# Relative attention: own scores of four units in one group, or of two pairs around the first transposes

## The chip, the cores and the metric

The kernel runs on one core of one Trainium2 chip. The metric is the device time of one execution, in microseconds (us). The profile comes from one more execution, taken by the hardware profiler; its span is the time from the first to the last instruction of the program.

## What is computed

The reference is a two-layer decoder on x of 4 batches x 512 positions x 128 features, in float32: per layer an attention, a cross attention and a feed-forward part with experts. Here one stage matters, the second layer's attention with relative positions: 16 heads of size 8, 512 queries and keys in each of 4 batches. In short:

```python
score_1 = einsum('bhqd,bhkd->bhqk', q_head, k_head)
score_2 = einsum('qmd,qkd->qmk', q_resh, rpk)      # rpk: rel_k by clipped distance q - k
scores  = (score_1 + score_2) / sqrt(D)
attn    = softmax(scores)
weight_1 = einsum('bhqk,bhkd->bhqd', attn, v_head)
weight_2 = einsum('qmk,qkd->qmd', se, rpv)         # rpv: rel_v by clipped distance
out = (weight_1 + weight_2) @ Wo.T + bo
```

## The kernel before

The program is written per engine: each engine has its own list of instructions in a fixed order, and semaphores (the table SD) hold them to each other. Stages A to G follow one another; stage D, the relative attention, is `pe_D` on TensorE, `act_D` on ScalarE, `dve_D` on VectorE and `pool_D` on GpSimd.

Stage D handles four units at a time. Q counts these groups, 16 to a batch (w = Q % 16) and 64 in all. A unit k = 4Q + j has its scores, 128 rows x 512 keys in float32, in one PSUM bank, and the banks go round in a ring of five: unit k has bank k % 5. So a unit's scores may be written only when the exp of unit k - 5 has read them.

TensorE does four things for a group, in `pe_D`:

- `scores(Q)`: 16 matmuls of the own scores (L1159), each on one 32x32 tile of the array. `e` is the unit, `c` the 32 output rows, and the input rows are `r = c ^ e`, so the 16 matmuls lie on 16 different tiles. Then four matmuls of the relative scores (L1169), two pairs (`par`), one unit on each half of the rows, which add into the same banks. Their semaphore `sc` tells VectorE that a pair is done. In front stands one wait: `exp` >= 4Q - 1, that is, until the third unit of the group before has been read.
- `flips(Q, 0)` and `flips(Q, 1)`: 16 transposes each (L1185), of the exps of the first and of the second pair of units. Each waits until the earlier half's transposes have been copied out, by ScalarE (`pta`) and by VectorE (`ptv`).
- `values(Q)`: 32 matmuls with the values (L1209) and 16 or 24 with the relative values (L1223).

The loop issues `scores(Q + 1)`, `flips(Q, 0)`, `values(Q - 1)`, `flips(Q, 1)`, one group ahead with the scores and one behind with the values. Once a batch, at w = 1, `spread_own` (L1239) and `spread_other` (L1251) come in, and the values move to the end.

ScalarE (L1279, L1290) does, for each Q: exp of unit 4Q+4, copy of the first transposes, exp of 4Q+5 and 4Q+6, copy of the second transposes, exp of 4Q+7. VectorE (L1321, L1329) does: top (negated maximum of a unit's scores) of 4Q+4 and 4Q+5, copy of the first transposes, top of 4Q+6, on even Q `pick` (L1337, L1341: two multiplies that take the values out of PSUM), top of 4Q+7, on even Q `add` (L1351), copy of the second transposes. Both take their half of each transposed block from its own PSUM bank. No DMA stands in this loop, except loads for the next batch on SP's queue.

Of the kernel before, what the change touches and what calls it, by code (L numbers as in the profile page):

```python
# [11 lines left out]
P = 128  # L12
B = 4
S = 512
# [30 lines left out]
RK0 = DK * (NU - 1) - REL0  # L45
# [43 lines left out]
def decoder(nc, t, out, last="G"):  # L89
# [3 lines left out]
    with ctx:  # L93
        def sb(name, shape, dt=F32):
            return ctx.enter_context(nc.sbuf_tensor(name, shape, dt))

        def sem(name):
            return ctx.enter_context(nc.semaphore(name))

        ps = ctx.enter_context(nc.psum_tensor("ps", [P, 8, 512], F32))  # L100
# [3 lines left out]
        w = {n: sqw[:, i, :] for i, n in enumerate(SQW)}  # L104
# [26 lines left out]
        rk = sb("rk", [P, RKW])  # L131
# [831 lines left out]
        def pool_C(pool):  # L963
# [8 lines left out]
            for n in range(NTT):  # L972
# [5 lines left out]
        SD = {n: sem("s_d_" + n) for n in ("qsp", "kst", "ldk", "ldv", "kp", "kt", "qt", "v", "spill", "ld", "a", "rk", "rv", "sc", "max", "exp", "t", "pta",  # L978
                                           "ptv", "pv", "oex", "sum", "rin", "ee", "r", "yn", "y2", "yst", "ao", "at")}
# [4 lines left out]
        NW = NU // 4  # L984
# [4 lines left out]
        AI = [a.rearrange("p (u n) -> p u n", u=QD) for a in (cw[:, 0:E1 * HID1],  # L989
                                                            cw[:, E1 * HID1:2 * E1 * HID1])]  # L990
# [16 lines left out]
        def unit_D(w, j):  # L1007

            z = j % 2
            return (2 * w + j // 2 if z == 0 else NU - 2 - 2 * w + j // 2), z  # L1010

        def tiles_D(w, z):

            n = 2 if w < NW // 2 else 3
            return list(range(n)) if z == 0 else list(range(NT - 1, NT - 1 - n, -1))

        NQ = B * NW
# [125 lines left out]

        def pe_D(pe):

            def scores(Q):
                b, w = Q // NW, Q % NW
                if w == 0:
                    if b:
                        pe.wait_ge(SD["ld"], LD * b)  # L1150
                    else:
                        pe.wait_ge(SD["ldk"], 32)
                    pe.wait_ge(SD["a"], 5 * (b + 1) + 1)
                if Q >= 1:
                    pe.wait_ge(SD["exp"], 4 * Q - 1)
                for e in range(4):
                    for c in range(4):
                        r, j = c ^ e, e
                        nc.tensor.matmul(ps[GW * c:GW * (c + 1), (4 * Q + j) % 5, :],  # L1159
                                         ALL[b % 2][GW * r:GW * (r + 1), j % 2, j // 2 * NW + w, :, :],  # L1160
                                         KT[b % 2][GW * r:GW * (r + 1), :], start=True, stop=False, skip_group_check=True,
                                         tile_position=(GW * r, GW * c))
                for par in range(2):
                    for z in range(2):
                        j = 2 * par + z
                        u = unit_D(w, j)[0]
                        k0, k1 = (0, min(S, 8 * u + 8 + P)) if z == 0 else (8 * u - P, S)
                        r0 = k0 - 8 * u + (RK0 if z == 0 else P)
                        nc.tensor.matmul(ps[:, (4 * Q + j) % 5, k0:k1], AI[b % 2][64 * z:64 * z + 64, par * NW + w, :],  # L1169
                                         rk[64 * z:64 * z + 64, r0:r0 + k1 - k0], start=False, stop=True,  # L1170
                                         skip_group_check=True).then_inc(SD["sc"], 1)

            def flips(Q, h):

                m = 2 * Q + h
                if m >= 1:
                    pe.wait_ge(SD["pta"], m)
                    pe.wait_ge(SD["ptv"], m)
                for j in range(2):
                    k = 2 * m + j  # L1180
                    pe.wait_ge(SD["exp"], k + 1)
                    for i in range(NT):
                        for z in range(2):
                            rows = slice(64 * z, 64 * z + 64)
                            ins = nc.tensor.transpose(ps[:, TB[z], j * 256 + i * 64:j * 256 + i * 64 + 64],  # L1185
                                                      PB[k % 6][rows, i * P:(i + 1) * P], c["ident"][rows, rows],
                                                      tile_position=(64 * z, 0))
                            if i == NT - 1:
                                ins.then_inc(SD["t"], 1)

            def values(Q):
                b, w = Q // NW, Q % NW
                q0 = 128 * (Q % 2)
                pe.wait_ge(SD["pta"], 2 * Q + 2)
                pe.wait_ge(SD["ptv"], 2 * Q + 2)
                if Q == 0:
                    pe.wait_ge(SD["ldv"], 16)
                    pe.wait_ge(SD["rv"], 2)
                if w == 0 and b >= 1:
                    pe.wait_ge(SD["yn"], 4 * b)  # L1200
                elif Q % 2 == 0 and Q:
                    pe.wait_ge(SD["oex"], Q)
                for h in range(2):
                    for t in range(NT):
                        for g in range(4):
                            j0, j1 = 2 * h, 2 * h + 1
                            m = PT[:, Q % 2, j0, t * P + GW * (g ^ j0):t * P + GW * (g ^ j0) + 1]
                            step = S + GW * (g ^ j1) - GW * (g ^ j0)
                            nc.tensor.matmul(ps[GW * g:GW * (g + 1), OBK, q0 + 64 * h:q0 + 64 * h + 64],  # L1209
                                             VT[b % 2][:, t * P + GW * g:t * P + GW * (g + 1)],  # L1210
                                             bass.AP(m.tensor, m.offset, [list(m.ap[0]), [step, 2], [1, GW]]),
                                             start=(t == 0), stop=(t == NT - 1), skip_group_check=True,
                                             tile_position=(0, GW * g))
                near = [tiles_D(w, z) for z in range(2)]
                n = len(near[0])
                for par in range(2):
                    for t in range(n):
                        for x4 in range(4):
                            z, ih = x4 // 2, x4 % 2
                            j = 2 * par + z  # L1220
                            u = unit_D(w, j)[0]
                            t0 = z * RVZ + (8 * u + S - P - P * near[z][t] - RV0) * DK + ih * GW
                            ins = nc.tensor.matmul(ps[GW * x4:GW * (x4 + 1), OBK, 256 + q0 + 64 * par:256 + q0 + 64 * par + 64],  # L1223
                                                   rv[:, t0:t0 + GW],
                                                   PT[:, Q % 2, j, near[z][t] * P:(near[z][t] + 1) * P]
                                                   .rearrange("p (h i) -> p h i", h=H)[:, :, 4 * ih:4 * ih + 4],
                                                   start=(t == 0), stop=(t == n - 1), skip_group_check=True,
                                                   tile_position=(0, GW * x4))
                            if t == n - 1 and par == 1:
                                ins.then_inc(SD["pv"], 1)  # L1230
# [15 lines left out]
            def spread_other(b):  # L1246

                pe.wait_ge(SD["ee"], 2 * b + 2)
                pe.wait_ge(SD["yn"], 4 * b + 1)
                for z in range(2):  # L1250
                    nc.tensor.matmul(ps[64 * z:64 * z + 64, OBK, :], rmask[:, :], E2R[:, z * S:(z + 1) * S],  # L1251
                                     start=True, stop=True, skip_group_check=True).then_inc(SD["r"], 1)

            scores(0)
            for Q in range(NQ):
                if Q + 1 < NQ:
                    scores(Q + 1)
                done = Q // NW - 1 if Q % NW == 1 and Q > 1 else None
                flips(Q, 0)
                if done is not None:  # L1260
                    spread_own(done)
                elif Q >= 1:
                    values(Q - 1)
                flips(Q, 1)
                if done is not None:
                    spread_other(done)
                    values(Q - 1)
# [1145 lines left out]
```

## Time and profile before

| | |
|---|---|
| time, median of 3 runs | 1510.87 us (1509.27 to 1512.24) |
| the profiled execution: its time | 1513.77 us |
| the profiled execution: its span | 1512.0 us |
| TensorE, VectorE, ScalarE busy, share of the span | 83%, 66%, 48% |
| granted clock of TensorE, mean | 0.93 |
| stage D | from 413 to about 812 us |

A busy share is a mean over seven stages with different limits. What a change in one stage is worth is read from that stage: from a table of stretches inside it, from the time line of one iteration, and from what ended the idle time of the engine in question. "issue" names idle time of an engine that waited for nothing that the profile shows. Ends of matmuls are modelled; their starts are recorded, so the text goes from start to start.

### The profile page before, as it was taken

Reading aid. Unit: us, or ns where it says so; the run is one execution under the profiler, and the core shown is the slowest. Engines: PE = TensorE matmul, PEld = TensorE weight load, DVE = VectorE, ACT = ScalarE, POOL = GpSimd, SP = SyncE. Lnnn points to the kernel's source line nnn. Section 1 sums busy time; section 2 is a strip of 40 time slices with the busy share of each in tenths; the row PEclk is TensorE's granted clock in tenths of the full one; section 3 lists DMA queues with packets and bytes.
Section 4 is the critical chain, followed back from the end, with each engine's and each line's share of the span. In section 5 each row is a group of like instructions: output and inputs, shape, how many; then the busy total and the mean of one; then the engine's idle time right before and its main releaser. Section 6 shows DMA issues by size and latency. Waiting matters only on the chain.

```text
span 1512.0 us, 46849 instructions
## 1 busy us (share of the span) xinstructions
PE 1250.1 (83%) x19471; PEld 796.5 (53%) x19471; DVE 991.6 (66%) x2513; ACT 730.2 (48%) x1814; POOL 236.7 (16%) x216
## 2 busy tenths in 40 slices
PE   4888888696479899898994889888988898889755
PEld 3443434285246666666663346634763476357544
DVE  4576676522558777777773678687858785778533
ACT  1323141442156666666661429543944394439334
POOL 2011121123030103131002030004000400030035
PEclk8989998898779999999996999999998999899878
DMA  9700000011440010110003200000000000000031
GB/s 323 286 8 9 17 1 8 9 55 46 157 159 4 11 39 5 26 24 11 11 5 80 53 1 2 4 1 15 3 4 1 14 3 2 1 15 3 4 101 49
DMA packets 56628, 59.27 MB, mean 39 GB/s; under 512 B 27854, under 2 KB 42065, under 8 KB 55265
## 3 DMA queue, kind: packets, MB, share of 16 engines
q1 hardware_dynamic: 51872, 47.82, 10.0%
q0 software_dynamic: 2528, 5.27, 1.1%
q8 instruction: 155, 2.54, 0.7%
q10 hardware_dynamic: 2016, 3.18, 0.6%
q14 instruction: 57, 0.46, 0.1%
HBM read 32.56 MB, written 24.14 MB: 38 GB/s over the span
## 4 chain that ended last, share of the span: by engine, by line
PE 54%; DVE 18%; ACT 11%; issue 8%; SPq 3%; DMA 3%; POOL 2%; ACTq 0%; POOLq 0%; DVEq 0%
PE ps L1159 5%; PE ps L271 5%; PE ps L1169 5%; DVE arena L620 4%; PE ps L1577 4%; PE ps L1185 4%; PE ps L492 3%; DVE arena L1730 3%; ACT arena L1668 3%; PE ps L1209 3%; PE ps L518 3%; DVE arena L1740 2%; PE ps L1632 2%; ACT arena L1678 2%; ACT arena L1279 2%
## 5 line engine op out<-in xcount | busy, mean ns | idle before, releaser
L1321 DVE TENSOR_REDUCE nmax<-ps 128x1 f32<-128x512 f32 x256 | 166.5, 682 | 70.4 <-PE ps L1169 70.4
L1668 ACT ACTIVATE arena<-ps,arena 128x512 f32<-128x512 f32 (+3 forms) x256 | 134.7, 539 | 74.4 <-DVE arena L1730 71.4
L1279 ACT ACTIVATE arena<-ps,nmax 128x512 f32<-128x512 f32 x172 | 118.9, 695 | 70.6 <-DVE nmax L1321 69.8
L1730 DVE TENSOR_REDUCE arena<-ps 128x1 f32<-128x512 f32 (+3 forms) x256 | 115.6, 484 | 15.1 <-PE ps L1592 13.5
L620 DVE TENSOR_REDUCE arena<-ps 128x8 f32<-128x1232 f32 x64 | 88.9, 1437 | 30.6 <-PE ps L480 30.6
L1329 DVE COPY arena<-ps 128x512 f32<-128x512 f32 x128 | 87.2, 682 | 22.5 <-PE ps L1185 22.3
L1740 DVE TENSOR_SCALAR arena<-arena 128x512 f32<-128x512 f32 (+3 forms) x256 | 92.0, 391 | 5.7
L1678 ACT COPY arena<-ps 128x512 f32<-128x512 f32 x160 | 85.9, 597 | 12.5 <-PE ps L1607 12.5
L271 PE MATMUL ps<-identb 128*128 128x512 bf16 x336 | 90.3, 428 | 1.4 <-DVE kcol L754 1.4
L1587 PE MATMUL ps<-arena 64*128 64x384 f32 (+3 forms) x512 | 88.3, 456 | 0.0
L1623 PE MATMUL ps<-arena 128*64 128x128 f32 x1280 | 87.8, 279 | 0.0
L1607 PE MATMUL ps<-sqc,arena 64*128 64x64 f32 x1280 | 67.1, 235 | 24.4 <-ACT arena L1678 11.4
L1290 ACT COPY arena<-ps 128x512 f32<-128x512 f32 x128 | 74.6, 583 | 24.7 <-PE ps L1185 23.4
L634 DVE TENSOR_TENSOR arena<-arena 128x512 f32<-128x512 f32 x96 | 62.8, 717 | 34.7 <-ACT arena L595 34.6
L1169 PEld LDWEIGHTS ps<-rk,cw 64*128 64x128 f32 x512 | 44.5, 192 | 61.0 <-issue 56.4
L1607 PEld LDWEIGHTS ps<-sqc,arena 64*128 64x128 f32 x1280 | 51.6, 138 | 46.1 <-ACT arena L1678 30.0
L1169 PE MATMUL ps<-rk,cw 64*128 64x168 f32 (+25 forms) x512 | 75.7, 414 | 0.0
L1623 PEld LDWEIGHTS ps<-arena 128*64 128x64 f32 x1280 | 68.5, 137 | 6.4
L1185 PE MATMUL ps<-sqc,arena 64*128 64x64 f32 x1376 | 62.7, 229 | 9.9 <-issue 7.1
L1159 PE MATMUL ps<-tmp,arena 32*32 32x512 f32 x1024 | 43.1, 642 | 31.4 <-DVE cw L1422 19.2
L475 PE MATMUL ps<-arena,q_t 32*128 32x320 f32 x512 | 52.5, 479 | 19.4 <-DVE arena L620 11.4
L1185 PEld LDWEIGHTS ps<-sqc,arena 64*128 64x128 f32 x1376 | 55.5, 142 | 21.2 <-issue 11.0
(354 smaller groups left out, 2574.5 us busy)
## 6 DMA issues: line engine op xcount, KB each, us to landing
xs_d<-onehot SPq DMA_DIRECT2D x4, 2560.0 KB, 26.4
cw<-in_cw SPq DMA_DIRECT2D x2, 2048.0 KB, 11.6
rv<-in_rv SPq DMA_DIRECT2D x2, 1536.0 KB, 16.5
late<-in_gw SPq DMA_DIRECT2D x3, 1024.0 KB, 10.6
arena<-gs_d SPq DMA_DIRECT2D x23, 129.0 KB, 2.1
onehot<-q_s SPq DMA_DIRECT2D x96, 8.0 KB
arena<-xs_d SPq DMA_DIRECT2D x23, 64.0 KB, 1.8
xs_d<-arena SPq DMA_DIRECT2D x23, 64.0 KB, 1.6
```

What stands on the lines that cost most here:

```text
L271: nc.tensor.matmul(ps[:, FILL[k][1], :].rearrange("p (a n) -> p a n", a=NT), identb[:, :], identb[:, :].unsqueeze(1).to_broadcast([P, NT, ...
L620: nc.vector.tensor_reduce(top_x[:, i, :, 2 * hp:2 * hp + 2], ps[:, bank:bank + NG4, 0:2 * KP].rearrange("p g (h k) -> p g h k", h=2)[:, :, ...
L1159: nc.tensor.matmul(ps[GW * c:GW * (c + 1), (4 * Q + j) % 5, :], ALL[b % 2][GW * r:GW * (r + 1), j % 2, j // 2 * NW + w, :, :], KT[b % 2][G ...
L1169: nc.tensor.matmul(ps[:, (4 * Q + j) % 5, k0:k1], AI[b % 2][64 * z:64 * z + 64, par * NW + w, :], rk[64 * z:64 * z + 64, r0:r0 + k1 - k0], ...
L1185: ins = nc.tensor.transpose(ps[:, TB[z], j * 256 + i * 64:j * 256 + i * 64 + 64], PB[k % 6][rows, i * P:(i + 1) * P], c["ident"][rows, row ...
L1279: nc.scalar.activation(PB[k % 6], ps[:, k % 5, :], ACT.Exp, bias=nmax[:, u:u + 1], accum_out=rsum[:, b % 2, u:u + 1]).then_inc(SD["exp"], 1)
L1321: nc.vector.tensor_reduce(nmax[:, k % NU:k % NU + 1], ps[:, k % 5, :], AX.X, ALU.max, negate=True)\
L1607: ins = nc.tensor.transpose(ps[:, FTB[z], (NT * h + j) * KD:(NT * h + j + 1) * KD], TF["p%d" % (n % 2)][HALVES[z], h * S + j * P:h * S + ( ...
L1623: ins = nc.tensor.matmul(ps[HALVES[h], FOB[a % 2], i * P:(i + 1) * P], TF["v"][:, v0:v0 + KD], PTF[n % 2][h][:, c0 + j * P:c0 + (j + 1) * ...
L1668: ins = nc.scalar.activation(TF["p%d" % (n % 2)][:, h * S + c0:h * S + c1], ps[:, FSB[n % 2][h], c0:c1], ACT.Exp, bias=TF["nmax"][:, k8:k8 ...
L1730: ins = nc.vector.tensor_reduce(TF["nmax"][:, k8:k8 + 1], ps[:, FSB[n % 2][h], c0:c1], AX.X, ALU.max, negate=True)
L1740: ins = nc.vector.tensor_scalar(p[:, c0:c1], p[:, c0:c1], TF["rinv"][:, k8 + k:k8 + k + 1], None, ALU.mult)
```

## The change

`scores` takes a second argument, `par`, and does the own and the relative scores of one pair of units. The loop issues the first pair where the whole group stood, and the second pair between the values and the second transposes. Each pair waits for the exps that its own two banks need: count 4Q - 3 and count 4Q - 1.

```diff
-            def scores(Q):
+            def scores(Q, par):
                 b, w = Q // NW, Q % NW
-                if w == 0:
+                if w == 0 and par == 0:
...
-                if Q >= 1:
-                    pe.wait_ge(SD["exp"], 4 * Q - 1)
-                for e in range(4):
+                if Q:
+                    pe.wait_ge(SD["exp"], 4 * Q + 2 * par - 3)
+                for e in (2 * par, 2 * par + 1):
                     for c in range(4):
                         r, j = c ^ e, e
                         nc.tensor.matmul(ps[GW * c:GW * (c + 1), (4 * Q + j) % 5, :],
...
-                for par in range(2):
-                    for z in range(2):
-                        j = 2 * par + z
...
+                for z in range(2):
+                    j = 2 * par + z
...
-            scores(0)
+            scores(0, 0)
+            scores(0, 1)
             for Q in range(NQ):
                 if Q + 1 < NQ:
-                    scores(Q + 1)
+                    scores(Q + 1, 0)
                 done = Q // NW - 1 if Q % NW == 1 and Q > 1 else None
                 flips(Q, 0)
                 if done is not None:
                     spread_own(done)
                 elif Q >= 1:
                     values(Q - 1)
+                if Q + 1 < NQ:
+                    scores(Q + 1, 1)
                 flips(Q, 1)
```

## Rows read from the trace of the kernel before

**Rows 1.** The page, busy us, share of the span and instructions of each engine.

```profile
PE 1250.1 (83%) x19471; PEld 796.5 (53%) x19471; DVE 991.6 (66%) x2513; ACT 730.2 (48%) x1814; POOL 236.7 (16%) x216
```

**Rows 2.** Table by stretch: length, PE and PEld of L1159; last row all lines.

```profile
530.40:617.30 86.90, 20.05 (x480) 4.16 (x480) 1.00 0.09 19
626.70:709.80 83.10, 18.51 (x480) 3.92 (x480) 1.00 0.09 20
719.80:788.80 69.00, 15.99 (x384) 3.28 (x384) 1.00 0.04 8
...
sum 239.00, PE 220.02 PEld 156.70 DVE 180.78 ACT 161.09 POOL 26.52; mean PE 73.34 PEld 52.23 DVE 60.26 ACT 53.70 POOL 8.84
```

**Rows 3.** Time line, TensorE, one iteration: start, us, engine, line, instruction, count, idle before.

```profile
547.52 1.15 PE L1159 MATMUL ps<-q_t,arena 32*32 32x512 f32 x32 [0.47 <-ACT arena L1279]
548.60 1.07 PE L1169 MATMUL ps<-rk,cw 64*128 64x232 f32 x8
549.50 0.66 PE L1185 MATMUL ps<-sqc,arena 64*128 64x64 f32 x16
550.09 1.10 PE L1209 MATMUL ps<-arena,xn 128*32 128x64 f32 x64
551.01 0.63 PE L1223 MATMUL ps<-arena,rv 128*32 128x64 f32 x32
551.57 0.71 PE L1185 MATMUL ps<-sqc,arena 64*128 64x64 f32 x16
```

**Rows 4.** Time line, VectorE and ScalarE around the same iteration.

```profile
546.60 0.42 DVE L1337 TENSOR_TENSOR dec_row<-ps,m 128x256 f32<-128x256 f32 x1
...
547.27 0.68 DVE L1321 TENSOR_REDUCE nmax<-ps 128x1 f32<-128x512 f32 x1
547.87 0.67 DVE L1351 TENSOR_REDUCE arena<-dec_row 128x128 f32<-128x512 f32 x1
548.46 0.68 DVE L1329 COPY arena<-ps 128x512 f32<-128x512 f32 x1
...
549.34 1.29 DVE L1321 TENSOR_REDUCE nmax<-ps 128x1 f32<-128x512 f32 x2 [0.20 <-PE ps L1169]
550.06 0.69 ACT L1279 ACTIVATE rot<-ps,nmax 128x512 f32<-128x512 f32 x1 [1.30 <-DVE nmax L1321]
550.74 0.57 ACT L1290 COPY arena<-ps 128x512 f32<-128x512 f32 x1
...
551.88 0.69 ACT L1279 ACTIVATE arena<-ps,nmax 128x512 f32<-128x512 f32 x1
```

**Rows 5.** Time line, TensorE: the next group of own scores, cut in two.

```profile
552.72 0.15 PEld L1159 LDWEIGHTS ps<-q_t,arena 32*32 32x32 f32 x8 [0.57 <-ACT arena L1279]
552.72 1.99 PE L1159 MATMUL ps<-q_t,arena 32*32 32x512 f32 x32 [0.43 <-ACT arena L1279]
...
553.59 0.21 PEld L1159 LDWEIGHTS ps<-q_t,arena 32*32 32x32 f32 x24 [0.72 <-issue]
```

**Rows 6.** Time line, TensorE: an iteration late in the batch.

```profile
588.31 1.14 PE L1159 MATMUL ps<-q_t,arena 32*32 32x512 f32 x32
...
589.38 1.44 PE L1169 MATMUL ps<-rk,cw 64*128 64x344 f32 x8
...
591.24 1.10 PE L1209 MATMUL ps<-arena,xn 128*32 128x64 f32 x64
...
592.16 0.85 PE L1223 MATMUL ps<-arena,rv 128*32 128x64 f32 x48
...
592.94 0.71 PE L1185 MATMUL ps<-sqc,arena 64*128 64x64 f32 x16
```

**Rows 7.** TensorE's waits from 426 to 790 us: total us, times, longest us.

```profile
PE ps L1223 <- issue: 7.8, 10, 1.1
PE ps L1159 <- ACT arena L1279: 6.0, 16, 0.5
PE ps L1185 <- issue: 5.5, 9, 1.4
```

**Rows 8.** The page's DMA queues, the one of instructions: packets, MB, share of engines.

```profile
q8 instruction: 155, 2.54, 0.7%
```

More of the change, by code:

```diff
@@ L1162, in scores @@
                                          tile_position=(GW * r, GW * c))
-                for par in range(2):
-                    for z in range(2):
-                        j = 2 * par + z
[L1166 to L1171, printed above, removed]
+                for z in range(2):
+                    j = 2 * par + z
+                    u = unit_D(w, j)[0]
+                    k0, k1 = (0, min(S, 8 * u + 8 + P)) if z == 0 else (8 * u - P, S)
+                    r0 = k0 - 8 * u + (RK0 if z == 0 else P)
+                    nc.tensor.matmul(ps[:, (4 * Q + j) % 5, k0:k1], AI[b % 2][64 * z:64 * z + 64, par * NW + w, :],
+                                     rk[64 * z:64 * z + 64, r0:r0 + k1 - k0], start=False, stop=True,
+                                     skip_group_check=True).then_inc(SD["sc"], 1)
             def flips(Q, h):
```

## The prediction

> **What bounds the kernel now.** The page comes first: TensorE is busy for 83% of the span, VectorE for 66% [rows 1]. That is an average over stages, and the change touches one, the relative attention (stage D, from 413 to 812 us), so the next view is the table of stretches over its undisturbed parts. There the line of the own scores has 480, 480 and 384 MATMULs, 32 to one iteration (each fp32 matmul of the code is two of them): 15 + 15 + 12 = 42 iterations in 86.9 + 83.1 + 69.0 = 239.0 us, **5.69 us an iteration** [rows 2]. TensorE is busy in 220.0 of these 239.0 us. So all that any reordering can win here, without less TensorE work, is 19.0 / 42 = 0.45 us an iteration. The stage has 64 iterations, 61 of them in the steady loop: a ceiling of about 28 us.
>
> The third view is the time line of one undisturbed iteration, scores of w = 6 [rows 3]. From one start to the next: own scores (L1159) 1.08 us until L1169 begins, relative scores (L1169) 0.90, first transposes 0.59, values 0.92 and 0.56, second transposes 0.64 until the earliest start of the next scores, then 0.47 of waiting for ScalarE: 5.2 us. In a late iteration (w = 13) L1169 takes 1.27 (589.38 to 591.24 less 0.59) and L1223 0.78, and the second transposes end after 592.94 + 0.71 - 588.31 = 5.34 us, with the wait about gone [rows 6]. So the clean period is 5.20 to 5.34, mean 5.27, and the missing 0.42 of 5.69 is stalls: TensorE idles with nothing to wait for but "issue" [rows 7], and one of these cuts a score group in two [rows 5].
>
> The wait for ScalarE is a loop: end of the first relative scores, reduce_max (VectorE), exp, copy, exp, exp (ScalarE), next scores [rows 4]. Its largest row is 6.0 us in all [rows 7]. That loop is what the change loosens.
>
> **The change, part by part.** No instruction is added or removed; no DMA, no queue of SP or POOL is touched. Sixteen own-score matmuls and four relative ones become 8 + 2 ahead of the first transposes and 8 + 2 behind the values.
>
> *(a) The wait that it loosens.* The first pair waits for the exp of the first unit of the group before instead of the third; their exps start at 550.06 and 551.88, 1.8 us apart [rows 4]. The second pair waits for the third as before, but is issued a whole values block later. The 0.47 of the early iterations goes: at most 0.45 on average over all, with the stalls.
>
> *(b) The own scores in two halves.* The sixteen matmuls sit on sixteen different 32x32 tiles of the array and run side by side: 32 MATMULs in 1.15 us [rows 3]. A half uses eight tiles and leaves the other eight empty. What does it cost? Lower end: half the time, 0.54. Upper end: as long as the whole, 1.08. The nearest row is the group that a stall cut: its first four matmuls were loaded at 552.72, the other twelve at 553.59, so a quarter held TensorE for up to 0.87, and the group took 1.99 instead of 1.15 [rows 5]. Part of the 0.87 may be the stall itself, but it is nearer to the upper end, and L1169 (whose tiles overlap all of them) cannot start before the half has drained. I take **1.05 a half**, so 1.0 more TensorE time in each iteration.
>
> *(c) The relative scores in two halves.* Each half is half of 0.90 (early) or of 1.27 (late) [rows 3, 6] plus some 0.07 for a second start: 0.5 and 0.7.
>
> *(d) The new order on the other engines.* VectorE's program is unchanged: top, top, copy, top, [pick, on even Q], top, [add], copy. Its third top now waits for the second pair, which comes only after the values. Behind that top in VectorE's queue stands the second copy of the transposes, and TensorE's next first transposes wait for this copy. From the end S of the second pair, in an **even** iteration: 0.08 to the first top (no row has it alone; between the 0.04 from VectorE to ScalarE, 549.34 + 0.68 = 550.02 to 550.06, and the 0.15 below), 0.60 top, 0.67 pick, 0.60 top, 0.59 add, 0.68 copy, 0.15 to TensorE (exp ended 551.88 + 0.69 = 552.57, L1159 started 552.72) = **3.37** [rows 4, 5]. In an **odd** one, without pick and add: 2.11. ScalarE's copy: 0.08 + 0.68 + 0.04 + 0.68 (exp) + 0.58 + 0.15 = 2.21. Meanwhile TensorE has only the second transposes, then the next first pair: 0.64 + 1.05 + 0.5 = 2.19 early, 0.64 + 1.05 + 0.7 = 2.39 late. So it stands still for about 1.1 us in every even iteration and for nothing in an odd one. Before, the third top had its scores long before, and even so the copy of an even iteration ended at 548.46 + 0.68 = 549.14, only 0.36 ahead of the transposes at 549.50 [rows 3, 4]: there is no cover to spare.
>
> *(e) The sum of one iteration.* The rest of it, first transposes to the end of the second pair, is 0.59 + 0.92 + 0.56 + 1.05 + 0.5 = 3.62 early, and 0.59 + 0.92 + 0.78 + 1.05 + 0.7 = 4.04 late. Even and odd: 6.99 and 5.83 (early), 7.41 and 6.43 (late); mean of the four **6.66**, against 5.27 clean before.
>
> *(f) The stalls.* They follow the page's queue of instructions, 155 packets, 2.54 MB [rows 8]: about 64 bytes for each of TensorE's 2 x 19471 instructions [rows 1], so 16 KB every 256 of them, some 1.4 blocks an iteration. If they are code arriving late, a slower loop gives it more time, and the wait of (d) covers some. Bounds: none left (0), all left (0.42). I take half, 0.2.
>
> New iteration 6.86, old 5.69: 1.17 x 61 = **71 us**. The three boundaries between batches keep their order (their waits for POOL and VectorE are there before and after), and I count them as ordinary iterations. The profiled execution took 1513.77 us with a span of 1512.0; the median is 1510.87, so the difference goes onto the median as it is: 1510.9 + 71 = **1582 us**.
>
> On the stalls a page speaks against me. The Trainium skill, "Runtime: NRT & Kernel Launch", section "Instruction fetch mechanics", says that the fetch runs ahead and is hidden because the sequencer dispatches more slowly than blocks arrive. The trace does not agree as I read it: L1223 and L1185 idle for 7.8 and 5.5 us on "issue" [rows 7]. By the page the stalls would have another cause, and a slower loop would give nothing back.
>
> **The rivals.**
> - *All stalls stay*: 6.66 + 0.42 = 7.08, that is 1.39 x 61 = +85 us: 1596. The page above would have it so. Against it: a stall that falls where VectorE is late anyway costs nothing.
> - *VectorE is not late* (its copy gets in earlier than I count, or TensorE is so much slower that it always finds it done): even iterations are as odd ones, 5.81 early and 6.43 late, 6.12 + 0.2 = 6.32, +0.63 x 61 = +38: 1549. Against it: the order of VectorE's program is fixed, and 3.37 against 2.19 is no close race.
> - *Half a group takes half the time*, 0.54: then 6.48 and 5.31 early, 6.90 and 5.74 late (VectorE 3.37 and ScalarE 2.21 set the first part), 6.11 + 0.2 = 6.31: 1549 as well, but with TensorE idle instead of busy. Against it: rows 5.
> - *Faster*: the halves take half the time and the copy is not late, so only the loosened wait and a share of the stalls count. TensorE's work is then 4.7 early, 5.3 late, with 0.1 for the second start 5.1, with 0.2 of stalls 5.3: -0.39 x 61 = -24: 1487. It decides at the point where splitting adds less than about 0.4 us an iteration. For it: TensorE does wait for ScalarE in half of the iterations. Against it: two things of (b) and (d) would have to be wrong at once.
>
> **How the numbers follow.** Chances: forecast (1560 to 1600) 0.62, all stalls stay 0.10, VectorE not late 0.12, half the time 0.09, faster 0.05, about no change 0.02. The range from 1545 to 1605 takes in the forecast, the two cases at 1549 and the stalls in full, and leaves out the faster end and anything beyond a second wait that I do not see. Faster by over 0.2% (about 3 us, what a measurement of this kernel can tell from no change) 0.05, within it 0.02, slower 0.93.
>
> **What the changed profile would show.** (b): the line of the own scores in groups of 16 MATMULs, each about 1.05 until L1169's successor line starts; its busy time near double; about 0.55 would be the half-time rival. (d): a wait of the first transposes for VectorE's copy of some 1 us in every second iteration, 30 us or so in all, that was not there; no wait of the own scores for exp. (f): fewer "issue" gaps at the values. The prediction is wrong if TensorE's busy time in the stage hardly grows, or if the period stays under 6 us.

## The result and the profile after

| | before | after |
|---|---|---|
| time, median | 1510.55 us (1509.27 to 1512.24) | 1598.39 us (1596.46 to 1608.03) |
| ratio to before, 95% interval | | 1.0594 [1.055, 1.0637] |
| profiled execution: time, span | 1513.77, 1512.0 us | 1598.32, 1596.5 us |

The change costs 88 us. The prediction said 71 and 1582; the measured time lies inside the range from 1545 to 1605, near its upper end.

The same three undisturbed parts of the stage answer to [rows 2]: table by stretch, length, then busy time and count of TensorE's MATMULs and weight loads of L1159; the last row is that of all lines.

```profile
546.60:654.60 108.00, 34.79 (x480) 5.72 (x480) 1.00 0.07 16
665.90:771.50 105.60, 33.65 (x480) 5.50 (x480) 1.00 0.07 16
784.40:869.40 85.00, 29.23 (x384) 4.72 (x384) 1.00 0.03 7
...
sum 298.60, PE 264.57 PEld 157.60 DVE 176.80 ACT 160.38 POOL 26.44; mean PE 88.19 PEld 52.53 DVE 58.93 ACT 53.46 POOL 8.81
```

The counts are the same, 15 + 15 + 12 iterations, and they take 298.6 us instead of 239.0: 7.11 us each instead of 5.69. The line of the own scores is busy for 97.7 us instead of 54.6 (34.79 + 33.65 + 29.23 against [rows 2]) for the same 1344 MATMULs, and TensorE as a whole for 264.6 instead of 220.0. TensorE's idle time has grown too, from 19.0 to 34.0 us.

One even iteration, on the time line, shows both (TensorE and VectorE; line numbers have moved by one to three: L1168 are the relative scores, L1184 the transposes, L1208 and L1222 the values; on VectorE L1323 is a top, L1331 the copy).

```profile
564.60 1.09 PE L1159 MATMUL ps<-q_t,arena 32*32 32x512 f32 x16
...
565.62 0.64 PE L1168 MATMUL ps<-rk,cw 64*128 64x224 f32 x4
...
566.34 0.69 DVE L1323 TENSOR_REDUCE nmax<-ps 128x1 f32<-128x512 f32 x1 [1.94 <-PE ps L1168]
...
566.69 1.09 PE L1159 MATMUL ps<-q_t,arena 32*32 32x512 f32 x16
566.95 0.41 DVE L1339 TENSOR_TENSOR dec_row<-ps,m 128x256 f32<-128x256 f32 x1
...
567.61 0.68 DVE L1323 TENSOR_REDUCE nmax<-ps 128x1 f32<-128x512 f32 x1
...
567.70 0.68 PE L1168 MATMUL ps<-rk,cw 64*128 64x232 f32 x4
...
568.21 0.67 DVE L1353 TENSOR_REDUCE arena<-dec_row 128x128 f32<-128x512 f32 x1
...
568.80 0.68 DVE L1331 COPY arena<-ps 128x512 f32<-128x512 f32 x1
...
569.58 0.72 PE L1184 MATMUL ps<-sqc,arena 64*128 64x64 f32 x16 [1.21 <-issue]
```

A half of 16 MATMULs takes 1.02 us until the relative scores begin (564.60 to 565.62, 566.69 to 567.70); the whole of 32 took 1.08 [rows 3]. Behind the second pair VectorE does top, pick (two steps), top, add and copy; the copy ends at 568.80 + 0.68 = 569.48, and the first transposes begin at 569.58. TensorE's 1.21 us of idle time before them is named "issue" here, but it ends 0.10 after that copy. From the end of the second pair before it (565.62 + 0.64 = 566.26) to these transposes it is 3.32 us, where (d) counted 3.37. In the table of waits it is the largest row. Of its 31 times 30 fall in the even iterations, one in each from the scores of Q = 4 to 62, 35.8 us in all; the one left, 0.4 us, falls in an odd one:

```profile
PE ps L1184 <- issue: 36.2, 31, 1.7
PE ps L1222 <- issue: 8.5, 7, 1.4
```

The wait of the own scores for ScalarE [rows 7] is not among TensorE's waits any more. So the loosened wait is gone as planned. It was 6.0 us [rows 7] and 2.3 more of the same wait in the row below, which names another tile:

```profile
PE ps L1159 <- ACT rot L1279: 2.3, 5, 0.5
```

These 8 us are far less than what the two halves and the copy cost.

For the experiments an iteration is split into two numbers, worked out from the starts of L1159 in each trace: its **mean** over the 42 undisturbed iterations, and its **clean** length, the mean over the same iterations of the shortest one of the four batches at the same w (without the first batch at w = 0 and 1, which has no values to do yet). The difference is the **stall**. Before: mean 5.69, clean 5.26, stall 0.43. After: 7.11, 6.63, 0.48. Each number comes from one trace; in each of the three parts by itself the stall is 0.28 to 0.54 before and 0.42 to 0.58 after.

### The profile page after: what moved, and what is told of

Its sections match the earlier page's. It is cut to its first block, busy times and chain, and to the rows that moved or that the text cites. A ratio compares the mean times of both kernels' runs of the same rounds, so it can differ in the third digit from the quotient of the medians.

```text
span 1596.5 us, 46849 instructions
## 1 busy us (share of the span) xinstructions
PE 1317.8 (83%) x19471; PEld 796.9 (50%) x19471; DVE 989.5 (62%) x2513; ACT 731.5 (46%) x1814; POOL 236.9 (15%) x216
## 4 chain that ended last, share of the span: by engine, by line
PE 59%; DVE 17%; issue 9%; ACT 7%; SPq 2%; POOL 2%; DMA 2%; ACTq 0%; POOLq 0%; DVEq 0%
PE ps L1159 8%; PE ps L1168 5%; PE ps L271 5%; PE ps L1208 4%; DVE arena L620 4%; PE ps L1184 4%; PE ps L1579 3%; PE ps L492 3%; ACT arena L1670 3%; DVE arena L1732 3%; PE ps L518 2%; PE ps L1222 2%; DVE arena L1742 2%; PE ps L1634 2%; PE ps L1625 2%
## 5 line engine op out<-in xcount | busy, mean ns | idle before, releaser
L1323 DVE TENSOR_REDUCE nmax<-ps 128x1 f32<-128x512 f32 x256 | 167.0, 684 | 182.9 <-PE ps L1168 182.6
L1168 PEld LDWEIGHTS ps<-rk,cw 64*128 64x128 f32 x512 | 39.3, 187 | 115.0 <-issue 115.0
L1168 PE MATMUL ps<-rk,cw 64*128 64x168 f32 (+25 forms) x512 | 92.7, 436 | 3.5 <-issue 3.5
L271 PE MATMUL ps<-identb 128*128 128x512 bf16 x336 | 94.1, 441 | 1.4 <-DVE kcol L754 1.4
L1159 PE MATMUL ps<-tmp,arena 32*32 32x512 f32 x1024 | 74.2, 616 | 21.3 <-DVE cw L1424 19.6
L1331 DVE COPY arena<-ps 128x512 f32<-128x512 f32 x128 | 86.8, 678 | 4.1 <-PE ps L1184 4.1
L1609 PE MATMUL ps<-sqc,arena 64*128 64x64 f32 x1280 | 67.7, 236 | 23.7 <-DVE arena L1742 10.6
L1184 PE MATMUL ps<-sqc,arena 64*128 64x64 f32 x1376 | 60.5, 226 | 27.5 <-issue 27.0
L1184 PEld LDWEIGHTS ps<-sqc,arena 64*128 64x128 f32 x1376 | 54.9, 140 | 47.6 <-issue 36.4
L1159 PE MATMUL ps<-q_t,arena 32*32 32x512 f32 x1024 | 75.8, 607 | 2.4 <-issue 2.4
## 6 DMA issues: line engine op xcount, KB each, us to landing
cw<-in_cw SPq DMA_DIRECT2D x2, 2048.0 KB, 11.4
```

Of the source, the lines that this page charges most:

```text
L271: nc.tensor.matmul(ps[:, FILL[k][1], :].rearrange("p (a n) -> p a n", a=NT), identb[:, :], identb[:, :].unsqueeze(1).to_broadcast([P, NT, ...
L1323: nc.vector.tensor_reduce(nmax[:, k % NU:k % NU + 1], ps[:, k % 5, :], AX.X, ALU.max, negate=True)\
L1609: ins = nc.tensor.transpose(ps[:, FTB[z], (NT * h + j) * KD:(NT * h + j + 1) * KD], TF["p%d" % (n % 2)][HALVES[z], h * S + j * P:h * S + ( ...
```

## The experiments

**e1: both halves in front.** Only the split is left of the change; the place of the second pair is undone.

```diff
                 if Q + 1 < NQ:
                     scores(Q + 1, 0)
+                    scores(Q + 1, 1)
...
-                if Q + 1 < NQ:
-                    scores(Q + 1, 1)
                 flips(Q, 1)
```

> Both pairs of scores, each as in the change, stand in front of the first transposes; only the split into two halves is left of the change, and VectorE has all four tops early again. Theory (a half of the own scores holds TensorE about as long as the whole, 1.0 us, since the eight other tiles stay empty): iteration early 1.02 + 0.5 + 1.02 + 0.5 + 0.59 + 0.92 + 0.56 + 0.64 = 5.75, late 6.37, mean 6.06, with the stalls of 0.42 as before and after 6.48 against 5.69: +0.79 x 61 = +48 us, 1559; no wait of 1 us at the first transposes. Rival (all of the loss is VectorE's lateness, halves cost half): 1510 to 1515.

Measured: 1546.59 us (1543.75 to 1552.96), ratio 1.0241 [1.0204, 1.0278]. Time line, TensorE, one iteration (w = 6, as in [rows 3]):

```profile
553.17 1.09 PE L1159 MATMUL ps<-q_t,arena 32*32 32x512 f32 x16
554.18 0.68 PE L1168 MATMUL ps<-rk,cw 64*128 64x232 f32 x4
554.79 1.09 PE L1159 MATMUL ps<-q_t,arena 32*32 32x512 f32 x16
555.81 0.67 PE L1168 MATMUL ps<-rk,cw 64*128 64x240 f32 x4
556.31 0.66 PE L1184 MATMUL ps<-sqc,arena 64*128 64x64 f32 x16
556.90 1.10 PE L1208 MATMUL ps<-arena,xn 128*32 128x64 f32 x64
```

Each half is 1.01 or 1.02, the relative pairs 0.61 and 0.50, and nothing waits: the transposes follow at once. Clean 6.07 us where 6.06 was expected: each half costs about as much as the whole did, and the split costs 0.81 us an iteration, net of the wait for ScalarE that goes with it. The rival "half the time" is out. The total is 12 us under the expected 1559, mainly because the stalls are 0.14 here, not 0.42.

**e2: VectorE's copy first.** The changed kernel, with one move in VectorE's list (the copy before the pick, the fourth top and the add).

```diff
                     top(4 * Q + 6)
+                copy(2 * Q + 1)
                 if Q % 2 == 0 and Q:
                     pick(Q - 1)
...
-                copy(2 * Q + 1)
```

> The changed kernel, with VectorE's copy of the second transposes moved ahead of pick, the fourth top and add. Theory (in even iterations TensorE's first transposes wait 1.0 to 1.2 us for this copy): the wait goes, even iterations become like odd ones, 30 x 1.15 = 35 us less than the changed kernel, 1563. Rival (that idle time has another cause, for the trace calls it issue): no change, 1598.

Measured: 1556.72 us (1548.04 to 1558.74), ratio 1.028 [1.0241, 1.032]. TensorE's wait before the transposes falls from 36.2 us in 31 to

```profile
PE ps L1184 <- issue: 1.3, 2, 0.7
```

so the idle time called "issue" was the wait for this copy. Clean 6.06 instead of 6.63: 0.57 an iteration, 35 us over 61. Fewer stalls (0.29) give another 12, and the three boundaries between batches take 4 back (13.3 us each, against 11.4 to 12.9).

**e3: the second pair amid the values.** The changed kernel, with the second pair of scores between the values (L1208) and the relative values.

```diff
-            def values(Q):
+            def values(Q, between=None):
...
+                if between is not None:
+                    scores(between, 1)
                 near = [tiles_D(w, z) for z in range(2)]
...
-                    values(Q - 1)
-                if Q + 1 < NQ:
+                    values(Q - 1, Q + 1 if Q + 1 < NQ else None)
+                if Q + 1 < NQ and (done is not None or Q == 0):
                     scores(Q + 1, 1)
```

> The changed kernel, with the second pair of scores between the values and the relative values instead of behind both. Two effects: the relative values (0.56 to 0.78 us) now stand between the second pair and the transposes that wait for VectorE, which covers so much of the wait in even iterations (about 30 x 0.65 = 20 us less); and the long run of dense instructions (first transposes, values, relative values, 224 to 256 instructions in 2.1 us) is cut in two. One more change of tile shape per iteration costs about 0.1 x 61 = 6. Theory that the stalls are code that arrives late where 256 instructions run by too fast: stalls per iteration fall from 0.42 to about 0.25, 10 us: 1574. Rival (stalls have nothing to do with how dense the instructions are): 1584. Rival (no cover): 1600.

Measured: 1564.86 us (1557.52 to 1566.79), ratio 1.0337 [1.0301, 1.0373]. The wait for the copy is partly covered, as expected:

```profile
PE ps L1184 <- issue: 15.5, 31, 1.0
```

But the clean iteration is 6.53, only 0.10 under the changed kernel's: what the cover gave was taken back in part. The values take 1.03 instead of 0.92 us with scores behind them; that the change of tile shape there is the reason was not tried by itself. What fell is the stall: 0.48 to **0.07**, where 0.25 was expected, so the time is 9 us under the expected 1574.

**e4: e2 and e3 together.**

```diff
...
+                if between is not None:
+                    scores(between, 1)
                 near = [tiles_D(w, z) for z in range(2)]
...
                     top(4 * Q + 6)
+                copy(2 * Q + 1)
...
-                copy(2 * Q + 1)
...
```

> e2 and e3 together. Theory: no wait for VectorE (1563) and fewer stalls (-10), one more change of tile shape (+6): 1559. Rival without the effect on stalls: 1569.

Measured: 1549.19 us (1547.0 to 1556.72), ratio 1.026 [1.022, 1.03]; clean 6.21, stall 0.02, and so 10 us under the expected 1559. With the changed kernel, e2 and e3 it makes a square, mean stall per iteration in us:

| | waits for VectorE's copy | does not wait |
|---|---|---|
| first transposes and all values in one run | 0.48 (after) | 0.29 (e2) |
| the run cut by the second pair | 0.07 (e3) | 0.02 (e4) |

**e5: VectorE's copy first, in the kernel before.** The diff is that of e2.

> The kernel before, with VectorE's copy of the second transposes moved ahead of pick, the third step of e2 alone. Theory: the copy was in time before (0.36 us ahead), so no change: 1508 to 1513. Rival (VectorE's lateness costs something in the kernel before as well): 10 us or more less.

Measured: 1512.41 us (1511.67 to 1514.2), with the kernel before at 1506.69 on the same chip: ratio 1.0042 [1.0026, 1.0059], a little slower rather than unchanged. Its clean iteration is 5.44 instead of 5.26 and its stall 0.18 instead of 0.43; the boundaries between batches take 12.2, 12.7 and 10.6 us instead of 8.7, 9.4 and 10.0. VectorE was in time in the kernel before, so the move gains nothing there. By the order of VectorE's list, a copy that must wait for the second transposes now holds up the fourth top, and behind it the exps; this was not tried by itself, but TensorE's wait for the exps has doubled, from 8.3 us to 16.7 (the row below and 4.8 in 9 for the tile `rot`):

```profile
PE ps L1159 <- ACT arena L1279: 11.9, 24, 0.6
```

TensorE's list is here the same as in the kernel before, and its stalls are 0.25 less all the same.

**e6: the code moved by up to 96 places.** The changed kernel with 96 waits, met at once, ahead of the stage's first scores.

```diff
+            for _ in range(96):
+                pe.wait_ge(SD["rk"], 2)
             scores(0, 0)
```

> The changed kernel with 96 waits that are met at once, in TensorE's list ahead of the stage's first scores: the same work, its instructions moved by up to 96 places against the blocks of 256 in which code is fetched. Theory (stalls are late code): the stalls of 1 to 2 us come at other places of the loop (other iterations or other lines) than in the changed kernel, with about the same sum; time within 8 us of 1598. Rival (they belong to the work, such as a collision with other engines or loads): the same iterations and lines stall.

Measured: 1597.58 us (1595.37 to 1602.72), stall 0.44; the 96 waits show as 48 more records in the trace. Time line of the changed kernel, TensorE, the iteration whose scores have 296 columns:

```profile
595.55 0.78 PE L1168 MATMUL ps<-rk,cw 64*128 64x296 f32 x4
597.43 0.46 PE L1184 MATMUL ps<-sqc,rot 64*128 64x64 f32 x8 [1.10 <-issue]
...
598.07 1.10 PE L1208 MATMUL ps<-arena,xn 128*32 128x64 f32 x64
598.99 0.73 PE L1222 MATMUL ps<-arena,rv 128*32 128x64 f32 x38
601.13 0.41 PE L1222 MATMUL ps<-arena,rv 128*32 128x64 f32 x10 [1.40 <-issue]
601.47 1.09 PE L1159 MATMUL ps<-q_t,arena 32*32 32x512 f32 x16
```

and of e6, the same iteration:

```profile
593.22 0.78 PE L1168 MATMUL ps<-rk,cw 64*128 64x296 f32 x4
595.10 0.46 PE L1184 MATMUL ps<-sqc,rot 64*128 64x64 f32 x8 [1.10 <-issue]
...
595.74 1.10 PE L1208 MATMUL ps<-arena,xn 128*32 128x64 f32 x64
596.65 0.85 PE L1222 MATMUL ps<-arena,rv 128*32 128x64 f32 x48
597.44 1.09 PE L1159 MATMUL ps<-q_t,arena 32*32 32x512 f32 x16
```

The wait for VectorE's copy (1.10) stays where it was, to the hundredth. The stall of 1.40 in the middle of the relative values is gone from this iteration. Two iterations on, at the scores of 328 columns, both kernels stall, at different places. In e6 it is again in the middle of the relative values:

```profile
606.94 0.83 PE L1168 MATMUL ps<-rk,cw 64*128 64x328 f32 x4
608.83 0.72 PE L1184 MATMUL ps<-sqc,arena 64*128 64x64 f32 x16 [1.05 <-issue]
...
610.39 0.61 PE L1222 MATMUL ps<-arena,rv 128*32 128x64 f32 x27
611.92 0.53 PE L1222 MATMUL ps<-arena,rv 128*32 128x64 f32 x21 [0.92 <-issue]
```

In the changed kernel the relative values of this iteration run through, and the gap comes in the own scores behind them, 24 matmuls and 24 weight loads later, which is the 48 records:

```profile
614.47 0.85 PE L1222 MATMUL ps<-arena,rv 128*32 128x64 f32 x48
615.25 1.04 PE L1159 MATMUL ps<-q_t,arena 32*32 32x512 f32 x3
616.60 1.08 PE L1159 MATMUL ps<-q_t,arena 32*32 32x512 f32 x13 [0.31 <-issue]
```

The same word in the same column thus has two causes, and the shift tells them apart: one belongs to the work, the other to the place in the code. A count says the same. Number TensorE's records (matmuls, weight loads and those of its sequencer) from 0 in order of time, and look at its "issue" gaps of over 0.3 us from Q = 19 to 62. Those that are no wait for the copy (which stands ahead of the first transposes of an even iteration) come at number 193 or 194 modulo 256: 12 of 12 in the kernel before, 12 of 12 in the changed one, 9 of 9 in e6. The waits for the copy, 21 in the changed kernel and 21 in e6, come at other numbers, all over the 256. A gap of the first kind ends 2.2 to 3.0 us after a 16 KB packet of the instruction queue [rows 8] starts, a wait for the copy anywhere from 1.8 to 6.3 us after one.

**e7 and e8: a try at gaining from it.** From the kernel before: the sixteen own scores stay one group in front, only the second relative pair moves to between the values and the relative values; e8 has VectorE's copy first as well.

```diff
-                for par in range(2):
+                relative(Q, 0)
+
+            def relative(Q, par):
...
+                if between is not None:
+                    relative(between, 1)
                 near = [tiles_D(w, z) for z in range(2)]
...
```

> From the kernel before: the sixteen own scores stay one group in front, with the first relative pair; only the second relative pair moves, to between the values and the relative values. It cuts the dense run (first transposes, values, relative values, second transposes, 256 to 288 instructions) as e3 did, without a second group of own scores. Theory (cutting the dense run takes away most stalls, the ScalarE loop then ends at the third top and exp, 1.5 us behind the second relative pair, about where TensorE arrives): clean iteration 5.2 to 5.5, stalls 0.1 instead of 0.43, VectorE late by 0.2 in even iterations: 1495 to 1505. Rival (stalls stay): 1515. Rival (the loop over the third exp becomes longer than I count, or VectorE's lateness of 3.37 us bites as in the change): 1520 to 1535.

> e7 with VectorE's copy of the second transposes ahead of pick, as in e2. Theory: VectorE is late in e7's even iterations by no more than 0.2 us, so at most 6 us less than e7. Rival (VectorE's lateness is as large as in the change): some 20 us less than e7.

Measured: e7 1526.66 us (1523.05 to 1529.99), ratio 1.0135 [1.0112, 1.0158]; e8 1519.4 us (1514.31 to 1525.03), ratio 1.0081 [1.0055, 1.0108], the kernel before at 1506.46. The stalls did go, to 0.10 and 0.05, as the theory of e7 had it. But the clean iteration of 5.2 to 5.5 and the 1495 to 1505 us expected of e7 are missed: the clean iteration rose from 5.26 to 5.75 (e7) and 5.66 (e8). The values take 1.03 us instead of 0.92 with relative scores behind them, the two relative pairs by themselves more than together, and the ScalarE loop is still there:

```profile
PE ps L1159 <- ACT arena L1287: 10.2, 32, 0.6
```

e8 is 7 us faster than e7 where at most 6 was expected. Neither beats the kernel before. By the means of the traces e7's iteration is only 0.16 longer (5.85 against 5.69), about 10 us of its 20; the rest is not accounted for.

## Why the prediction was right, and where it was off

| step | predicted | measured |
|---|---|---|
| (a) the wait for exp goes | yes | none left among TensorE's waits |
| (b) one half of the own scores | 1.05 us | 1.02 |
| (c) one relative pair, early and late | 0.5, 0.7 | 0.48 to 0.67, 0.66 to 0.69 |
| (d) VectorE's copy late, even iterations | about 1.1 us, 30 times | 35.8 us in 30 |
| (e) even and odd, early | 6.99, 5.83 | 7.09, 5.89 |
| (e) even and odd, late | 7.41, 6.43 | 7.51, 6.32 |
| (e) clean iteration, mean | 6.66 | 6.63 |
| without (d): splitting alone | 6.12 | 6.07 (e1), 6.06 (e2) |
| (f) stalls | 0.2 | **0.48** |

The measured pairs are the clean lengths at w = 6, 5, 12 and 13. The parts of the loss, clean, over 61 iterations: splitting 6.07 - 5.26 = 0.81, 49 us (e1); VectorE's copy 6.63 - 6.06 = 0.57, 35 us (e2); stalls 0.48 - 0.43, 3 us. That is 87 of 88; the spans of the two traces differ by 84.5 us, so it is no closer than some 3 us.

The number of (b) came out, but the row under it did not bear on it: the group in [rows 5] is cut at number 194 modulo 256, so its 0.87 us is mostly a stall of the kind that e6 moves, and says little of what a part of a group costs. That 1.05 was near is in this part luck. Each tile has two MATMULs in a half (16 on 8 tiles) as in the whole (32 on 16), which fits 1.02 against 1.08; other parts of a group were not tried.

The step that failed is **(f)**. It took the stalls for code that arrives late, and e6 and the count bear that out. From this it concluded that a slower loop would halve them, and here it did not: the loop became 25% slower, and the stalls are 0.48 against 0.43, no less than before. With 0.48 in the place of 0.2 the sum is 6.63 + 0.48 = 7.11, 1.42 x 61 = 87; the 0.28 are 17 us, all of what the forecast fell short by. What the runs show in its place: cutting the stretch of first transposes and values in two takes the stalls away, whether TensorE waits for the copy (0.48 to 0.07) or not (0.29 to 0.02). The change left this stretch in one piece. The same count names the packet of each block of 256 records, since every gap of this kind ends at the block whose packet is the last to have started. In the ten traces, 60 blocks in each, no block's first record starts sooner than 2.15 us after its packet, and the packet mostly starts after TensorE has begun the block before it, at the median 1.17 us after that in the kernel before and 1.14 in the changed one. So a block that would run through in less than about 3.3 us (an estimate, 2.15 + 1.14) tends to end in a stall, whatever time the rest of the iteration takes.

The rival "all stalls stay" (1596) therefore gave the best number, with a cause that the runs do not support. By the Trainium skill, "Runtime: NRT & Kernel Launch", section "Instruction fetch mechanics", fetching is hidden behind the dispatch. The runs do not agree for this stage: the stalls move with the code (e6), and they cost about 0.43 x 61 = 26 us in the kernel before. The other rivals fell: "VectorE is not late" by e2, "half the time" by e1, and "faster" by both.

A smaller slip: the prediction counted the boundaries between batches as ordinary iterations. They went from 8.7, 9.4 and 10.0 to 11.5, 11.4 and 12.9 us, 1.1 more each than an ordinary iteration; the start of the stage is 3 us shorter, and its end 3 us longer, so it hardly shows in the sum.

What stays open: why e1, whose dense stretch is as long as that of the kernel before, has stalls of 0.14, and e5, whose list on TensorE is that of the kernel before, 0.18. So the length of the stretch does not decide alone, and a longer iteration may have helped in e1 as (f) thought. Waits do not order the runs either: they go with more stalls in the square, and with fewer in e5. In e1 the packets start sooner after the block before has begun, at the median 0.78 us instead of 1.17; what makes them do so, no run shows.

## What to carry to other kernels

Matmuls that fill the array side by side must be split only if the parts stay full: half of a packed group takes as long as the whole, here 1.02 us against 1.08. Before a producer is moved later to free an engine, follow the consumer's list past the instruction that now waits: here it was the copy, with pick, top and add between it and the top that now waits, and it cost 35 us. And when the trace says "issue", look at what ended 0.1 us earlier; if nothing did, number the engine's records to see whether the gaps keep a fixed distance of 256, and shift the code to see whether they move.

## What the hardware showed that was not expected

Late code does not cost by the mean rate alone: the changed kernel fetches its 16 KB blocks at a lower mean rate than the kernel before (60 packets in 315 us, Q = 19 to 62, against 60 in 252) and stalls as much, while cutting one stretch of 224 to 256 instructions (matmuls and weight loads: 32 of the first transposes, 128 of the values, 64 to 96 of the relative values) into two brings 0.48 us an iteration down to 0.07 (e3), and 0.29 down to 0.02 (e4). A dense stretch is not enough by itself: e1 has one of 256 to 288 and stalls of 0.14. Cutting it has its own price in this kernel, 0.4 to 0.5 us an iteration in e7 and e8, so the stalls are cheaper than that cure.
